# Six DRAM-to-DRAM copies of expert weights moved from SyncE's queue to ScalarE's queue

## The chip, the cores and the metric

One Trainium2 chip, of which the program uses one core. The metric is the device time of one execution in microseconds (us). Before the change three runs gave 1790.77, 1791.66 and 1792.70 us, median 1791.66.

## The reference

A stack of four layers on `x` (8 x 256 tokens of width 256), each an attention to a context of 120 rows and then a feed-forward block. Each block is added to `x` after a layer norm of its input. Cut to the two blocks that the change touches, the first feed-forward block and the last:

```python
def _L0_ffn_ref(oldx, W_in, b_in, W_out):          # 8 trees of 255 nodes
    logits = x @ W_in.T + b_in
    decisions = (logits > 0)
    acts = silu(logits)
    ...                                            # dmap: the nodes on each token's path
    return (acts * dmap).reshape(B, WIDTH) @ W_out.T

def _L3_ffn_ref(x, Wg, bg, W1, b1, W2, b2):        # 8 experts, one for each token
    probs = softmax(x @ Wg + bg)
    assignments = argmax(probs)
    h = gelu(x @ W1[e] + b1[e])
    eo = h @ W2[e] + b2[e]                         # e = assignments
    return probs[assignments] * eo
```

Between them lie attention and feed-forward blocks of layers 1 and 2 and the attention of layer 3.

## The kernel before

The eight blocks run one after the other as phases 0 to 7, each over four pairs of batches (512 tokens a pair) in a hardware loop `Fori(0, PAIRS)`. Every engine has its own instruction stream, written by hand, and the streams meet at semaphores. `x` stays in SBUF from start to end.

SyncE (SP in the profile) issues nearly all transfers, in program order. First come the loads of the first phases and the small weights of later ones (L380 to L420). Then for each attention phase it waits until the phase starts and issues masks and contexts.

The second feed-forward block (layer 2's, phase 5) uses big weights, `f1T`, `f2T`, `h1T` and `h2T`, and the last block uses expert weights. Both sets are first copied from the inputs to buffers in DRAM, and are loaded from there to SBUF when their place is free.

- `copy_f1T`, `copy_f2T`, `copy_h1T`, `copy_h2T` (1, 1, 4 and 4 MB) are issued by ScalarE (ACT) at L1203, behind its work for phase 0 and ahead of its work for phase 1. They raise the semaphore `w_copied`. SyncE waits for it (L438) before it loads them at the start of phase 2.
- `kits` (in the trace `copy_experts`), for each of 8 experts a block of 128 rows that holds its two matrices and two biases, is filled by SyncE at L457 to L462, in six copies: `w1e` in two, `w2e` in two, `b1e` and `b2e`. They stand at the end of phase 4's transfers, behind the load of `h2w` (L454) and behind the 17 MB that set the routing buffer `xbuf` to zero (L456). They raise `Hf.zeroed`. SyncE waits for it before the job loads (L470), GpSimd before it scatters the routed rows, both in phase 7.

A copy of `w1e` or `w2e` takes a slice `a[w][:, k*128:(k+1)*128, :]`, 8 experts x 128 rows x 1 KB, into rows of `kits`; `b1e` is 8 x 128 pieces of 8 bytes, and `b2e` 8 x 128 rows of 1 KB.

Phase 1, the tree block, is where ScalarE's order matters. For tree p and half c (nodes 0 to 126, nodes 127 to 254) TensorE makes logits (L1495), VectorE makes `dec` (L685), ScalarE the silu `act` (L1214), TensorE counts how many decisions agree (L1504), VectorE makes `msk` (L677) and TensorE multiplies by `woutT` (L1512). Logits lie in two sets of PSUM banks, so TensorE's stream has for tree p, ahead of its logits:

```python
if p >= 2:
    pe.wait_ge(Bf.act, i * (2 * TREES) + (2 * p - 2))
```

that is, tree 2's logits wait for both silus of tree 0. ScalarE's own stream, around the place of the change, is: the evacuations of phase 0's last `xT` (L1183, L1184), the four copies at L1203, then the silus of phase 1.

Of the kernel before, what the change touches and what calls it, by code (L numbers as in the profile page):

```python
# [17 lines left out]
B, S, D, SK = 8, 256, 256, 120  # L18
# [4 lines left out]
K2 = D // 128  # L23
# [4 lines left out]
NE = 8  # L28
# [9 lines left out]
W1, W2, B1, B2, KIT = 0, K2 * D, 2 * K2 * D, 2 * K2 * D + K2, 2 * K2 * D + K2 + D  # L38
# [31 lines left out]
def build(nc, a, out, phases=8):  # L70
# [224 lines left out]
    def sem(name):  # L295
        return es.enter_context(nc.semaphore(name))
# [4 lines left out]
    ld_h1, w_copied = sem("ld_h1"), sem("w_copied")  # L301
# [22 lines left out]
    Hf = Signals()  # L324
# [23 lines left out]
    def next_pair(i):  # L348
        return (i + 1) % PAIRS

    def rows(i, n=TT):

        return x[:, ds(TT * i, n), :]
# [6 lines left out]
    proj = {"l1x": None, "l2x": (wq2, wk2, wv2, wo2), "l3x": (wq3, wk3, wv3, wo3)}  # L360

    LD_CONST, LD_L0, LD_IN, LD_OUT, LD_L1 = 8 * 16, 5 * 16, 2 * 16, 3 * 16, 7 * 16
    W_COPIED = 4 * 16
    ZEROED = (1 + 2 * K2 + 2) * 16
    LD_L2, LD_L3X, LD_L3 = (5 + 3 + 2 * 2 + 2) * 16, 4 * 16, 2 * 16

    w_in = {w: nc.dram_tensor("copy_" + w, [m, HID], F32, kind="Internal").ap()
# [1 line left out]
    kits = nc.dram_tensor("copy_experts", [NE, 128, KIT], F32, kind="Internal").ap()  # L369
# [7 lines left out]
    def _(sp):  # L377
# [23 lines left out]
        def next_context(i):  # L401
            sp.dma_start(ctxp[:], kp(a["ctxT"][:, ds(next_pair(i) * (2 * SK), 2 * SK)])).then_inc(ctx_ready, 16)
# [18 lines left out]
        for L in LAYERS:  # L421
            if phases <= L.phase:
                break
            s = X[L.name]
            if L is L3X:
                sp.wait_ge(Ff.p1, PAIRS * HT)
                sp.dma_start(wq3[:], kp(a["wq3"])).then_inc(ld_l3x, 16)
                sp.dma_start(wk3[:], kp(a["wk3"])).then_inc(ld_l3x, 16)
                sp.dma_start(wv3[:], kp(a["wv3"])).then_inc(ld_l3x, 16)
                sp.dma_start(wo3[:], kp(a["wo3"])).then_inc(ld_l3x, 16)  # L430
            sp.wait_ge(res_done, 4 * L.phase + 1)
            sp.wait_ge(wrcp, 1)
            if L is L3X:
                sp.dma_start(wg[:], kp(a["wg"])).then_inc(ld_l3, 16)
                sp.dma_start(bgB[:], a["bg"].partition_broadcast(128)).then_inc(ld_l3, 16)
            elif L is L1X:
                sp.dma_start(m32[:], a["mask"][0:TOK, :].rearrange("(t p) k -> p t k", p=128)).then_inc(mask_ready, 16)
                sp.wait_ge(w_copied, W_COPIED)  # L438
                sp.dma_start(f1, kp(w_in["f1T"])).then_inc(ld_h1, 16)
                sp.dma_start(f2, kp(w_in["f2T"])).then_inc(ld_h1, 16)  # L440
                sp.dma_start(h1w[:], kp(w_in["h1T"])).then_inc(ld_h1, 16)
            with sp.Fori(0, PAIRS) as i:
                if L is not L3X:
                    sp.wait_ge(s.mb, i + 1)
                    sp.dma_start(m32[:], a["mask"][ds(next_pair(i) * TOK, TOK), :]
                                 .rearrange("(t p) k -> p t k", p=128)).then_inc(mask_ready, 16)
                sp.wait_ge(s.kp, i + L.c0 + 1)
                sp.wait_ge(s.vp, i + L.c0 + 1)
                next_context(i)
            if L is L2X and phases > 5:  # L450

                sp.wait_ge(mask_ready, 16 * 9)
                sp.wait_ge(res_done, 4 * 5 + 1)
                sp.dma_start(h2w[:], kp(w_in["h2T"])).then_inc(ld_h2, 16)  # L454
                sp.wait_ge(filled, 1)
                sp.dma_start(xbuf.rearrange("(p r) c -> p r c", p=128),  # L456
                             zeros[:].unsqueeze(1).broadcast_to([128, SLOTS // 128, CELL])).then_inc(Hf.zeroed, 16)  # L457
                for c, w in ((W1, "w1e"), (W2, "w2e")):
                    for k in range(K2):
                        sp.dma_start(kits[:, :, c + k * D:c + (k + 1) * D], a[w][:, k * 128:(k + 1) * 128, :]).then_inc(Hf.zeroed, 16)  # L460
                sp.dma_start(kits[:, :, B1:B1 + K2], a["b1e"].rearrange("p (e k) -> e p k", e=NE)).then_inc(Hf.zeroed, 16)
                sp.dma_start(kits[:, :, B2:B2 + D], a["b2e"].unsqueeze(1).broadcast_to([NE, 128, D])).then_inc(Hf.zeroed, 16)  # L462

        def job_weights(j, e):
            sp.dma_start(jw[:, j % NB, :], kits[ds(e, 1), :, :].rearrange("e p n -> (e p) n")).then_inc(ld_job[j % NB], 16)
# [1 line left out]
        def job_rows(j, row):  # L467
            sp.dma_start(jx[:, j % NB, :], xbuf[ds(row, 128), :]).then_inc(ld_job[j % NB], 16)

        sp.wait_ge(Hf.zeroed, ZEROED)  # L470
        sp.wait_ge(Hf.tab, 1)
        for j in range(NB):
            job_weights(j, sp.value_load(jtab[0:1, 1, j:j + 1], min_val=0, max_val=NE - 1))
# [7 lines left out]
        for load, total in ((ld_x, 16), (ld_x_rest, 16), (ld_const, LD_CONST), (ld_l0, LD_L0), (ld_in, LD_IN), (ld_out_w, LD_OUT),  # L481
                            (ld_l1, LD_L1), (ld_l2, LD_L2), (mask_ready, (0, 16 * 5, 16 * 9)[sum(phases > q for q in (2, 4))]),
                            (w_copied, W_COPIED), (ld_h1, 48 if phases > 2 else 0), (ld_h2, 16 if phases > 5 else 0), 
                            (ld_l3x, LD_L3X if phases > 6 else 0), (ld_l3, LD_L3 if phases > 6 else 0),
# [4 lines left out]
            sp.wait_ge(ld_job[b], LD_JOB * ((JOBS - 1 - b) // NB + 1))  # L489
        for b in range(NO):  # L490
            sp.wait_ge(st_job[b], 16 * ((JOBS - 1 - b) // NO + 1))
        sp.wait_ge(Hf.zeroed, ZEROED)

# [1 line left out]
    @block.gpsimd  # L497
    def _(pool):
        pool.memset(mhalf[:], -0.5)
        pool.memset(ceps[:], LN_EPS)  # L500
        pool.memset(ones[:], 1.0)
        pool.memset(zeros[:], 0.0)
        pool.drain().then_inc(filled, 1)
        pool.sem_inc(res_done, 1)

        def rstd_of(n):

            pool.wait_ge(ln_var, n)
            pool.tensor_tensor(veps[:], mv[:, :, 1], ceps[:], ALU.add)  # L509
            pool.drain()  # L510
            pool.tensor_tensor(rstd[:], veps[:], mhalf[:], ALU.pow).then_inc(ln_rstd, 1)

        rstd_of(1)

        for p in range(phases - 1):
            with pool.Fori(0, PAIRS) as i:
                if p in (4, 6):

                    if p == 4:
                        pool.wait_ge(ld_l2, LD_L2)  # L520
                    pool.wait_ge(xln_ready, 4 * p + i + 1)
                    pool.tensor_tensor(rows(i), rows(i), boB[:, p // 2 - 2, :].unsqueeze(1).broadcast_to([128, TT, D]),
                                       ALU.add).then_inc(X["l2x"].bo, 1)
                rstd_of(i + (4 * p + 2))

        pool.iota(acc[:, 0, :], pattern=[[PLACES // 128, NE]], base=0, channel_multiplier=0,
                  allow_small_or_imprecise_dtypes=True)
        pool.iota(tokc[:], pattern=[[128, NT]], base=1, channel_multiplier=1, allow_small_or_imprecise_dtypes=True)
        pool.iota(starts[:], pattern=[[PLACES, NE]], base=0, channel_multiplier=0,
                  allow_small_or_imprecise_dtypes=True)  # L530
        pool.iota(jrow[:], pattern=[[1, JOBS], [0, NE]], base=0, channel_multiplier=0,
                  allow_small_or_imprecise_dtypes=True)
        pool.memset(csum[:], 0.0)
        pool.memset(oh[:], 0.0)
        pool.memset(cells[:, :, D:CELL], 0.0)
        pool.memset(onesb[:], 1.0)
        pool.memset(tri[:], 1.0)
        pool.drain()
        pool.affine_select(tri[:], tri[:], pattern=[[1, 128]], compare_op=ALU.is_gt, fill=0.0, base=0,
                           channel_multiplier=-1)  # L540
        pool.drain().then_inc(Hf.consts, 1)

        def send(i):
            pool.wait_ge(Hf.place, i + 1)
            pool.wait_ge(Hf.cells, i + 1)
            for t in range(TT * i, TT * i + TT):
                pool.indirect_dma_start(xbuf[:], bass.IndirectOffsetOnAxis(placei[:, t:t + 1], 0), cells[:, t, :], None,
                                        bounds_check=SLOTS - 1, oob_is_err=False).then_inc(Hf.sent, 16)

        pool.wait_ge(Hf.zeroed, ZEROED)  # L550
        rstd_of(4 * 7 + 2)
        rstd_of(4 * 7 + 3)
        send(0)
        rstd_of(4 * 7 + 4)
        for i in range(1, PAIRS):
            send(i)
        for j in range(JOBS):
            pool.wait_ge(Hf.out, j + 1)
            pool.indirect_dma_start(out[:], bass.IndirectOffsetOnAxis(jtok[:, j % NO:j % NO + 1], 0), jout[:, j % NO, :],
                                    None, bounds_check=B * S - 1, oob_is_err=False).then_inc(st_job[j % NO], 16)  # L560
# [614 lines left out]
    def _(act):  # L1175
# [25 lines left out]

        for w, copy in w_in.items():
            act.dma_start(copy, a[w]).then_inc(w_copied, 16)  # L1203

        if phases > 1:
            with act.Fori(0, PAIRS) as i:
# [787 lines left out]
```

## Time and profile before

| what | us |
|---|---|
| median of three runs | 1791.66 |
| the profiled execution | 1792.70 |
| its span, first to last instruction | 1790.7 |
| TensorE busy | 1496.2 (84%) |
| ScalarE busy | 728.9 (41%) |
| phase 1 (trees), from about | 77 to 320 |
| phase 5 (layer 2's feed-forward), from about | 926 to 1310 |

The profile divides the span into 40 slices of 44.8 us and gives each engine's busy share in tenths. DMA issues are not counted as busy time of an engine: they stand in the timeline under the queue's name (ACTq, SPq), with the time for which the issue held that engine's instruction stream, which is not the time that the data took. A landing time is counted from the issue to the data's arrival.

### The profile page before, as it was taken

To read this page: it belongs to the slowest core of one execution; us is meant where nothing else is said; L and a number is where in the kernel's file an instruction comes from. 1 tells how busy PE (TensorE), PEld (TensorE's weight loads), DVE (VectorE), ACT (ScalarE), POOL (GpSimd) and SP (SyncE) were. 2 spreads that over 40 slices of the span, in tenths; PEclk is the share of its full clock that TensorE was granted. 3 is DMA by queue.
4 is the path that set the end of the run, shared out by engine and by line. 5 is a ranking of instruction groups with operands and counts; after the bars stand their busy time and mean duration, and the time that the engine had idled before them with its cause. 6 is when DMAs were issued, how large, how long until landed. Compare 5 with 4: busy or idle time off the path is not lost.

```text
span 1790.7 us, 25936 instructions
## 1 busy us (share of the span) xinstructions
PE 1496.2 (84%) x8925; PEld 1083.2 (60%) x8925; DVE 1062.5 (59%) x2273; ACT 728.9 (41%) x1214; POOL 103.0 (6%) x129
## 2 busy tenths in 40 slices
PE   6999999777779876787779999999988888888446
PEld 5665666555544443665566778787847484847345
DVE  3434434688777655778778161616167777775434
ACT  2312121456555654545442122222228474757122
POOL 0000000000000000001000000000000000000233
PEclk9999999888889997989989999999999899989579
DMA  9340000400000000000029500000000000000077
GB/s 322 104 141 0 0 0 0 158 12 11 11 0 1 1 1 12 12 3 8 11 98 342 163 1 2 1 2 2 31 6 2 6 0 5 0 5 0 22 250 232
DMA packets 56607, 88.58 MB, mean 49 GB/s; under 512 B 10419, under 2 KB 48428, under 8 KB 56366
## 3 DMA queue, kind: packets, MB, share of 16 engines
q1 hardware_dynamic: 54142, 72.08, 12.7%
q10 hardware_dynamic: 512, 11.11, 1.8%
q0 software_dynamic: 1872, 4.27, 0.6%
q8 instruction: 57, 0.93, 0.2%
q14 instruction: 24, 0.20, 0.0%
HBM read 65.74 MB, written 38.35 MB: 58 GB/s over the span
## 4 chain that ended last, share of the span: by engine, by line
issue 44%; PE 33%; DVE 9%; ACT 4%; DVEq 4%; DMA 2%; POOL 1%; ACTq 1%; SPq 1%; POOLq 0%
PE bank L1757 6%; PE bank L1758 6%; PE bank L1820 3%; PE bank L1577 3%; DVE plo L823 3%; PE bank L1597 2%; PE bank L1579 2%; DMA jx<-copy_routed 2%; PE bank L1531 2%; PE bank L1689 1%; ACT hq L1324 1%; ACTq L1323 1%; ACT phi L1265 1%; PE bank L1714 1%; DVEq L1018 1%
## 5 line engine op out<-in xcount | busy, mean ns | idle before, releaser
L823 DVE TENSOR_TENSOR plo<-e,phi 120x512 f16<-120x512 f32 x256 | 185.5, 741 | 85.7 <-ACT phi L1265 80.0
L1597 PE MATMUL bank<-Q,Kpad 128*120 128x256 f16 x1024 | 209.3, 287 | 8.6 <-ACT MBT L1257 8.6
L1271 ACT ACTIVATE e<-bank 120x512 f32<-120x512 f32 x256 | 152.7, 597 | 67.6 <-PE bank L1602 37.4
L778 DVE TENSOR_REDUCE MB<-bank 128x4 bf16<-128x480 f32 x256 | 149.9, 650 | 17.9 <-PE bank L1579 11.8
L1265 ACT ACTIVATE phi<-e 120x512 f16<-120x512 f32 x256 | 158.1, 623 | 0.0
L1577 PE MATMUL bank<-Kpad,Q 128*128 128x480 f16 x256 | 108.5, 424 | 56.3 <-issue 32.5
L1601 PE MATMUL bank<-MBT,selm 128*120 128x256 bf16 x512 | 143.8, 281 | 0.0
L1602 PE MATMUL bank<-MBT,sels 128*120 128x256 bf16 x512 | 143.8, 281 | 0.0
L1620 PE MATMUL bank<-V,phi 120*128 120x34 f16 (+1 forms) x1024 | 85.4, 176 | 56.1 <-DVE plo L823 55.0
L1597 PEld LDWEIGHTS bank<-Q,Kpad 128*120 128x120 f16 x1024 | 117.3, 138 | 10.7 <-ACT MBT L1257 10.7
L1495 PE MATMUL bank<-xT,winT 128*127 128x512 f32 (+1 forms) x256 | 114.8, 594 | 4.7 <-ACTq L1185 4.7
L1620 PEld LDWEIGHTS bank<-V,phi 120*128 120x128 f16 x1024 | 69.2, 96 | 80.0 <-DVE plo L823 71.7
L1512 PE MATMUL bank<-woutT,msk 128*128 128x256 f32 (+1 forms) x512 | 115.1, 379 | 0.0
L1577 PEld LDWEIGHTS bank<-Kpad,Q 128*128 128x128 f16 x256 | 27.7, 108 | 134.3 <-issue 73.3
L1757 PE MATMUL bank<-hah,h1w 128*128 128x512 f32 x256 | 102.4, 400 | 5.8 <-DVE hal L607 3.3
L1579 PE MATMUL bank<-MB,identb 128*128 128x480 bf16 x256 | 106.9, 418 | 0.0
L1512 PEld LDWEIGHTS bank<-woutT,msk 128*128 128x128 f32 (+1 forms) x512 | 97.2, 190 | 16.0
L1214 ACT ACTIVATE act<-bank,bin 127x512 f32<-127x512 f32 x64 | 44.0, 687 | 151.2 <-DVE dec L685 143.7
L1757 PE MATMUL bank<-hb,h2w 128*128 128x512 f32 x256 | 101.0, 395 | 0.8 <-DVE longw L1037 0.8
L1758 PE MATMUL bank<-hal,h1w 128*128 128x512 f32 x256 | 101.0, 395 | 0.0
L1758 PE MATMUL bank<-hbl,h2w 128*128 128x512 f32 x256 | 100.7, 393 | 0.0
L509 POOL TENSOR_TENSOR veps<-mv,ceps 128x4 f32<-128x4 f32 x32 | 6.4, 200 | 1573.3 <-DVEq L574 1447.0
(270 smaller groups left out, 2907.8 us busy)
## 6 DMA issues: line engine op xcount, KB each, us to landing
copy_routed<-zeros SPq DMA_DIRECT2D x1, 17028.0 KB
jw<-copy_experts SPq DMA_DIRECT2D x23, 641.0 KB, 4.8
h1w<-copy_h1T SPq DMA_DIRECT2D x1, 4096.0 KB, 18.9
h2w<-copy_h2T SPq DMA_DIRECT2D x1, 4096.0 KB, 14.1
ctxp<-in_ctxT SPq DMA_DIRECT2D x13, 240.0 KB, 2.6
jx<-copy_routed SPq DMA_DIRECT2D x23, 132.0 KB, 4.9
m<-in_mask SPq DMA_DIRECT2D x9, 240.0 KB, 2.7
copy_experts<-in_w1e SPq DMA_DIRECT2D x2, 1024.0 KB
```

The costliest lines, as they stand in the source:

```text
L778: dve.tensor_reduce(MB[:, t, h0 // 8, SK + h0 % 8:SK + h0 % 8 + 4], bank[2 + n % 4][:, 0:4 * SK].rearrange("p (h k) -> p h k", h=4), AX.X, ...
L823: dve.tensor_tensor(plo[:, u % 3, :], e32[:, u % 3, :], phi[:, u % 3, :], ALU.subtract).then_inc(s.lo, 1)
L1265: act.activation(phi[:, u % 3, :], e32[:, u % 3, :], ACT.Copy).then_inc(s.phi, 1)
L1271: act.activation(e32[:, u % 3, :], bank[2 + u % 4][0:SK, :], ACT.Exp).then_inc(s.exp, 1)
L1512: last = pe.matmul(bank[t // 2][:, (t % 2) * D:(t % 2) * D + D], msk0[0:n, p % 2, c, tok(t)], woutT[0:n, 2 * p + c, :], start=(p == 0 and ...
L1577: pe.matmul(ps, Q2[:, g, tok(t)], Kpad[:, 0, r0:r0 + 4, g, b * SK:b * SK + SK], start=True, stop=False)
L1597: pe.matmul(ps, Kpad[:, v, r, g, b * SK:b * SK + SK], Q2[:, g, qs], start=(v == 0), stop=False)
L1601: pe.matmul(ps, selm[:], MBT[:, h // 8, qs], start=False, stop=False)
L1602: last = pe.matmul(ps, sels[:, h % 8, :], MBT[:, h // 8, qs], start=False, stop=True)
L1620: pe.matmul(ps, phi[:, u % 3, cols], rhs, start=True, stop=False)
L1757: pe.matmul(ps, w, hi, start=start, stop=False)
L1758: return pe.matmul(ps, w, lo, start=False, stop=stop)
```

## The change

The six copies that fill `kits` are issued by ScalarE, right behind the four copies at L1203, and no longer by SyncE. They raise `w_copied` in place of `Hf.zeroed`, whose waits come down to the one transfer that is left on it; the wait for `w_copied` at L438 goes up from four transfers to ten. Nothing else differs.

```diff
-    W_COPIED = 4 * 16
-    ZEROED = (1 + 2 * K2 + 2) * 16
+    W_COPIED = (4 + 2 * K2 + 2) * 16
...
                 sp.wait_ge(filled, 1)
                 sp.dma_start(xbuf.rearrange("(p r) c -> p r c", p=128),
                              zeros[:].unsqueeze(1).broadcast_to([128, SLOTS // 128, CELL])).then_inc(Hf.zeroed, 16)
-                for c, w in ((W1, "w1e"), (W2, "w2e")):
-                    for k in range(K2):
-                        sp.dma_start(kits[:, :, c + k * D:c + (k + 1) * D], a[w][:, k * 128:(k + 1) * 128, :]).then_inc(Hf.zeroed, 16)
-                sp.dma_start(kits[:, :, B1:B1 + K2], a["b1e"].rearrange("p (e k) -> e p k", e=NE)).then_inc(Hf.zeroed, 16)
-                sp.dma_start(kits[:, :, B2:B2 + D], a["b2e"].unsqueeze(1).broadcast_to([NE, 128, D])).then_inc(Hf.zeroed, 16)
...
-        sp.wait_ge(Hf.zeroed, ZEROED)
         sp.wait_ge(Hf.tab, 1)
...
-        sp.wait_ge(Hf.zeroed, ZEROED)
+        sp.wait_ge(Hf.zeroed, 16)
...
-        pool.wait_ge(Hf.zeroed, ZEROED)
+        pool.wait_ge(Hf.zeroed, 16)
...
         for w, copy in w_in.items():
             act.dma_start(copy, a[w]).then_inc(w_copied, 16)
+        for c, w in ((W1, "w1e"), (W2, "w2e")):
+            for k in range(K2):
+                act.dma_start(kits[:, :, c + k * D:c + (k + 1) * D], a[w][:, k * 128:(k + 1) * 128, :]).then_inc(w_copied, 16)
+        act.dma_start(kits[:, :, B1:B1 + K2], a["b1e"].rearrange("p (e k) -> e p k", e=NE)).then_inc(w_copied, 16)
+        act.dma_start(kits[:, :, B2:B2 + D], a["b2e"].unsqueeze(1).broadcast_to([NE, 128, D])).then_inc(w_copied, 16)
```

## Rows read from the trace of the kernel before

**Rows 1.** The page: TensorE's busy time, then tenths in 40 slices of the span.

```profile
PE 1496.2 (84%) x8925; PEld 1083.2 (60%) x8925; DVE 1062.5 (59%) x2273; ACT 728.9 (41%) x1214; POOL 103.0 (6%) x129
...
PE   6999999777779876787779999999988888888446
...
DMA  9340000400000000000029500000000000000077
```

**Rows 2.** Timeline of SyncE's queue from 920 us: start, time held, instruction.

```profile
926.55 0.37 SPq L454 DMA_DIRECT2D h2w<-copy_h2T  x1
926.97 0.69 SPq L456 DMA_DIRECT2D copy_routed<-zeros  x1
927.71 64.33 SPq L460 DMA_DIRECT2D copy_experts<-in_w1e  x2
992.08 13.14 SPq L460 DMA_DIRECT2D copy_experts<-in_w2e  x2
1005.66 6.48 SPq L461 DMA_DIRECT2D copy_experts<-in_b1e  x1
1012.20 6.03 SPq L462 DMA_DIRECT2D copy_experts<-in_b2e  x1
```

**Rows 3.** SyncE's queue, what it waited for: total us, times, longest.

```profile
SPq L432 <- DVEq L646: 263.2, 1, 263.2
SPq L427 <- PE bank L1758: 246.5, 1, 246.5
```

**Rows 4.** The tile `copy_experts`: ns held at each issue, least, median, most.

```profile
L460 SPq DMA_DIRECT2D copy_experts<-in_w1e x2: 6390/32146/57901, 927.7 to 985.6; - x2
L460 SPq DMA_DIRECT2D copy_experts<-in_w2e x2: 6264/6551/6838, 992.1 to 998.4; - x2
```

**Rows 5.** Windows: length, busy (count) of PE, PEld, DVE, ACT, POOL, clock, DMA share, GB/s.

```profile
80.00:111.50 31.50, 31.50 (x107) 19.24 (x106) 13.59 (x27) 8.00 (x12) 1.21 (x2) 1.00 0.90 300
...
985.60:992.00 6.40, 3.84 (x16) 3.25 (x17) 3.75 (x9) 1.27 (x3) 0.00 (x0) 0.80 1.03 318
992.00:1018.20 26.20, 26.20 (x115) 21.62 (x114) 0.77 (x2) 4.83 (x7) 0.00 (x0) 0.98 0.53 152
1018.20:1027.00 8.80, 8.80 (x42) 7.66 (x41) 0.00 (x0) 1.97 (x2) 0.00 (x0) 1.00 0.40 121
```

**Rows 6.** Timeline of ScalarE and its queue, 76 to 81 us.

```profile
76.70 0.59 ACTq L1203 DMA_DIRECT2D copy_f1T<-in_f1T  x1
...
78.59 0.76 ACTq L1203 DMA_DIRECT2D copy_h2T<-in_h2T  x1
79.75 0.69 ACT L1214 ACTIVATE act<-bank,bin 127x512 f32<-127x512 f32 x1 [3.27 <-DVE dec L685]
80.68 0.69 ACT L1214 ACTIVATE act<-bank,bin 128x512 f32<-128x512 f32 x1 [0.24 <-PE bank L1495]
```

**Rows 7.** DMA view of 76 to 115 us: packets and MB; landing.

```profile
q10 hardware_dynamic: 224, 10.49, 79.8%
...
copy_h2T<-in_h2T ACTq DMA_DIRECT2D x1, 32.9
```

**Rows 8.** Timeline of TensorE in phase 1.

```profile
84.35 3.60 PE L1495 MATMUL bank<-xT,winT 128*127 128x512 f32 x8
```

**Rows 9.** Windows around two idle stretches of TensorE.

```profile
327.00:331.70 4.70, 0.00 (x0) 0.01 (x1) 3.92 (x6) 2.81 (x4) 0.00 (x0) 0.89 1.02 413
331.70:337.50 5.80, 5.78 (x15) 2.19 (x16) 3.95 (x6) 0.00 (x0) 0.00 (x0) 0.50 1.02 410
337.50:341.00 3.50, 3.50 (x20) 1.51 (x18) 3.48 (x7) 2.52 (x4) 0.00 (x0) 1.00 0.88 305
927.80:931.40 3.60, 0.00 (x0) 0.01 (x1) 3.07 (x7) 0.00 (x0) 0.00 (x0) 0.53 0.86 321
931.40:934.80 3.40, 3.40 (x8) 2.73 (x9) 0.00 (x0) 0.00 (x0) 0.00 (x0) 0.50 1.02 414
```

**Rows 10.** TensorE's waits from 926 to 1030 us.

```profile
PE bank L1424 <- issue: 2.3, 1, 2.3
```

## The prediction

> **What bounds the kernel now.** I read the page first. TensorE is busy 84% of the span, and its row of tenths stands at 9 in all the slices of phase 1, so a microsecond that TensorE loses there is a microsecond of the total; the DMA row is near zero between its peaks, so the DMA engines bound nothing over the whole [rows 1]. Then I read the queue that is relieved, SyncE's, in the timeline and in its waits [rows 2, 3], to see what the six copies cost where they stand now; the windows over the same stretch, to see how fast they ran and what TensorE did meanwhile [rows 5]; and last the place they move to: ScalarE's queue, what its copies look like, and who waits for ScalarE there [rows 6 to 8].
>
> **What is removed.** SyncE is held by the six issues from 927.71 to 1018.23 us, 90.5 us in all [rows 2]. It then waits 246.5 us more, for the last h1 matmul, before the next thing it has to issue [rows 3]. So 90.5 us less on that queue make that wait longer and nothing else earlier: worth 0. Do the copies disturb TensorE? From 992.0 to 1018.2 only they are in flight, and TensorE is busy all 26.20 us at a granted clock of 0.98; from 1018.2 to 1027.0 it is busy all 8.80 us [rows 5]. Nothing to gain there. Ahead of them, from 985.6 to 992.0, TensorE is idle for 2.56 us, and one of its waits near there is 2.3 us with no releaser in the profile [rows 5, 10]. The end of the zero fill runs at that time at 318 GB/s, and the fill stays. I take 0 for the removal; the upper bound is in the last rival.
>
> **What is added: six issues on ScalarE.** A plain issue costs 0.59 to 0.76 us there [rows 6]. But these copies are no plain issues [rows 2, 4]. The first `w1e` copy held SyncE for 57.9 us, the next three 6.39, 6.26 and 6.84 (the two `w2e` are the least and the most of their row, and together 13.14), `b1e` 6.48 and `b2e` 6.03. The zero fill, itself accepted in 0.69 us, was ahead of the first. So an issue is accepted at once when nothing long is being queued, and otherwise holds its engine until the one ahead has been queued, and that in turn goes only as fast as data drain once the queue is full.
>
> How much fits? The five 1 MB copies are 5.25 MB. From 992.0 to the end 26.2 us at 152 GB/s and 8.8 at 121 moved, 3.98 + 1.06 = 5.04 MB [rows 5]. So when the second `w1e` issue returned at 992.0, 0.2 MB had moved, and of the copy before it about 0.84 MB was left: some 820 of its 1,024 rows of 1 KB fit into the queue; the issue returns when the rest of the copy ahead has gone. When the last issue returned at 1018.2, 1.06 MB was left, just its own copy.
>
> On ScalarE the same sequence stands behind the four weight copies. These are 224 packets for 10.49 MB [rows 7], so they take little room in a queue that counts pieces, which is why they held ScalarE so briefly. But they take long: the last lands 32.9 us after its issue, at 78.59 + 32.9 = 111.5 us [rows 6, 7], with the DMA engines 0.90 busy from 80.0 to 111.5 [rows 5]. A queue is drained in order, so nothing behind them moves until then. Step by step:
>
> - 79.4: the first `w1e` copy is issued, accepted in about 0.65 us, as the zero fill was. 80.0.
> - The second `w1e` is held until all but 820 rows of the first are gone: that needs the weight copies done (111.5) and 0.2 MB more, at 1.05 MB in 6.3 us some 1.2 us. 112.7.
> - The other four are held as before, where they took from 992.0 to 1018.2, 26.2 us. 138.9.
>
> ScalarE is free at 138.9 and not at 79.4; 59.5 us of a stream that has work to do.
>
> **Who waits.** Behind the six issues stand the silus of tree 0, which started at 79.75 and 80.68 [rows 6]. VectorE's `msk` for tree 0 waits for them, and so does TensorE's block of logits for tree 2, which ran at 84.35 [rows 8]. TensorE has logits for trees 0 and 1 and one count to do, and that is done by 84.35: from there it stands. The two silus, 0.69 us each and 0.1 for the hand-over, end at 140.3, and the logits for tree 2 start at 140.4. That is 140.4 - 84.35 = **56.0 us** later. After that every engine has the order it had, and TensorE is full again, so nothing is won back in phase 1; nor later, since no later work stands on a time that doesn't shift with it (all early loads landed long before, and SyncE had waited 263.2 us for phase 2 to start [rows 3]; the new copies land at about 138.9 + 8.8 = 147.7 us, before it needs `w_copied`).
>
> **The clock.** TensorE idles for 56 us. After idle stretches of 4.7 and 3.6 us the granted clock stood at 0.50, that is 1.2 of 2.4 GHz, for the next 5.8 and 3.4 us of full work, and then rose to 1.00 [rows 9]. Half of these times is lost: 2.9 and 1.7 us. In before that clock was 1.00 in all of this stretch [rows 5]. I take the middle, **2.3 us**.
>
> **Sum.** 56.0 + 2.3 = 58.3 us. The profiled execution took 1792.7 us; 1851.0. It was 1.0 us above the median of its runs (1791.66), so for a median I say **1850.0 us**. A difference under 0.2% (3.6 us) I call no change.
>
> **The rivals.**
>
> - *ScalarE's issues are short: no back-pressure there.* For it: all its copies so far were accepted in under 0.8 us, with 10 MB in flight [rows 6, 7]. Then the six cost 6 x 0.62 = 3.7 us, tree 0's silus end at 79.4 + 3.7 + 1.5 = 84.6 against 84.35: +0.3 us, 1792. Against it: those copies were few large pieces, while each of these is 1,024 small ones, and SyncE was held by the very same ones. The Trainium skill ("DMA: Bandwidth & Descriptors", section "Issuing engines are not separate DMA queues") says for this case that a second issuing engine saves only the time to initiate the transfer, "which is usually small relative to the DMA itself"; by that rule the total would be this rival's, some 1792, and the trace speaks against it [rows 2], with holds of 6 to 58 us.
> - *ScalarE's queue is deeper by a copy.* The 0.84 MB is measured on SyncE's queue alone. With room for one copy more, each issue returns a copy (6.4 us) earlier: 1850.0 - 6.4 = 1843.6. For it nothing is seen; the two queues may differ.
> - *Each issue waits until everything ahead has moved.* Then ScalarE is free only at 111.5 + 6 x 6.4 = 149.9, the logits start at 151.4, 67.0 later, and with 2.9 for the clock it is 1861.6. Against it: at 992.0 and at 1018.2 about a copy was still outstanding.
> - *Faster.* The first rival holds, and phase 5 gets back what it lost around the copies: 2.6 us of idle TensorE from 985.6 to 992.0 and some 1.7 us of half clock behind it (0.80 in that window [rows 5], priced as above): 1792.7 + 0.3 - 4.3 - 1.0 = 1787.7. It decides only if ScalarE is held for less than the 3.0 us between the end of tree 0's second silu (80.68 + 0.69 = 81.37) and 84.35, and if the copies and not the fill made that idle time. The copies didn't start to move in bulk until about then. Improbable.
>
> That the change doesn't do its work is no case: the kits are in place long ahead of the jobs in either order.
>
> **How the numbers follow.** Forecast 0.70, deeper queue 0.12, waits for all 0.08, short issues 0.08, faster 0.02. The forecast's own bounds: the clock 0.6 us either way; the queue's share of the first copy, from none of it fitting (+5) to all of it (-1); and the weight copies' end, whose last engines set 111.5 while the mean DMA share in 80 to 111.5 is 0.90, so ScalarE's engines may be through up to 3 us earlier. Together 1845 to 1856. Taking in both neighbours gives 1842 to 1862, which leaves out 0.10 with the cases of no change. Slower 0.90, same 0.08, faster 0.02.
>
> **What would show it.** In the profile after, ScalarE's queue from 79.4 us: issues of about 0.6, 33, 6.4, 6.4, 6.8 and 6.3 us, in sum 59. TensorE idle for about 56 us from 84.8, ended by `act`, then a clock of 0.50 for 3 to 6 us. Phase 1's pace from tree to tree afterwards as before, and phases 2 to 7 the same in length. SyncE has no `copy_experts` writes around 930 to 1018, and TensorE there is as it was. Wrong would be: issues all under 1 us (then the queue isn't limited by pieces); a first long hold other than 33 us (then the weight copies don't stand in front); phases after that shorter or longer by more than 2 us (then the copies did disturb phase 5).

## The result and the profile after

| | median us | runs |
|---|---|---|
| before | 1792.18 | 4 (1790.77 to 1798.93) |
| after | 1849.44 | 4 (1846.72 to 1851.64) |

The ratio is 1.0311, 95% interval 1.0282 to 1.034: 57 us slower, where 58 were forecast (1850.0). The profiled execution after took 1848.59 us, its span is 1846.5 against 1790.7. Line numbers after are a few lower than before (L1494 is what was L1495, L1213 what was L1214).

The page after, TensorE's busy time and the tenths of TensorE and of the DMA engines. It answers to [rows 1]:

```profile
PE 1498.2 (81%) x8918; PEld 1081.7 (59%) x8925; DVE 1062.2 (58%) x2273; ACT 728.7 (39%) x1214; POOL 104.2 (6%) x129
...
PE   7709999977776986777877899999988888888446
...
DMA  9360000040000000000007700000000000000067
```

TensorE is busy for the same time as before (1498.2 against 1496.2 us) in a longer span. The third slice (92 to 138 us, the slices are 46.2 us long here) has gone from 9 to 0. In the same slice the DMA row has risen from 4 to 6, and of its peak in the middle, 2, 9 and 5 before, 7 and 7 are left.

The timeline of ScalarE and its queue, with the issues that answer to [rows 2] and [rows 6]:

```profile
78.45 0.81 ACTq L1196 DMA_DIRECT2D copy_h2T<-in_h2T  x1
79.29 31.23 ACTq L1199 DMA_DIRECT2D copy_experts<-in_w1e  x2
110.55 12.41 ACTq L1199 DMA_DIRECT2D copy_experts<-in_w2e  x2
122.99 6.23 ACTq L1200 DMA_DIRECT2D copy_experts<-in_b1e  x1
129.25 6.00 ACTq L1201 DMA_DIRECT2D copy_experts<-in_b2e  x1
135.51 2.42 ACT L1213 ACTIVATE act<-bank,bin 127x512 f32<-127x512 f32 x4 [59.20 <-issue]
```

The same tile by least, median and most ns of one issue:

```profile
L1199 ACTq DMA_DIRECT2D copy_experts<-in_w1e x2: 1287/15600/29912, 79.3 to 80.6; - x2
```

The last weight copy is accepted at 79.26. The first `w1e` copy held ScalarE 1.29 us, the second 29.9, the two `w2e` copies 6.2 each, `b1e` 6.23 and `b2e` 6.00. ScalarE is free at 135.25 and does the four silus that had piled up back to back, 2.42 us. The DMA view from 108.5 us to 110.52, when the second `w1e` issue came back, shows how much of the kit copies had started by then:

```profile
DMA packets 174, 0.16 MB, mean 80 GB/s; under 512 B 16, under 2 KB 174, under 8 KB 174
```

That is 158 rows of 1 KB and 16 short packets. So 866 of the 1,024 rows of the first `w1e` copy were still outstanding, where the prediction had 820.

TensorE, and what ended its idle time:

```profile
83.76 0.60 PE L1503 MATMUL bank<-dec,anc 127*127 127x512 bf16 x2
136.83 5.17 PE L1494 MATMUL bank<-xT,winT 128*127 128x512 f32 x8 [52.48 <-ACT act L1213]
141.84 0.60 PE L1503 MATMUL bank<-dec,anc 127*127 127x512 bf16 x2
142.28 3.62 PE L1511 MATMUL bank<-woutT,msk 127*128 127x256 f32 x16
145.73 3.60 PE L1494 MATMUL bank<-xT,winT 128*127 128x512 f32 x8
```

The block of 8 at 136.83 is the logits for tree 2, which ran at 84.35 before [rows 8]. Its one new wait in phase 1 is 52.5 us, and `act` ended it. The block took 5.17 us where the same one takes 3.60. The windows say why; the columns are those of [rows 5], the granted clock is the third from the right:

```profile
84.30:110.00 25.70, 0.05 (x1) 0.00 (x0) 0.00 (x0) 0.00 (x0) 0.00 (x0) 0.58 0.89 293
110.00:136.80 26.80, 0.00 (x0) 0.00 (x0) 0.48 (x1) 1.29 (x3) 0.00 (x0) 0.50 0.54 158
136.80:139.80 3.00, 2.97 (x4) 1.42 (x5) 0.93 (x2) 1.13 (x2) 0.00 (x0) 0.50 0.55 170
139.80:143.00 3.20, 3.20 (x11) 1.72 (x11) 1.28 (x2) 1.37 (x2) 0.00 (x0) 0.99 0.46 139
...
1040.00:1047.00 7.00, 4.18 (x18) 3.48 (x19) 4.10 (x10) 1.51 (x3) 0.00 (x0) 0.81 0.85 263
1047.00:1073.00 26.00, 26.00 (x115) 21.45 (x114) 0.42 (x1) 4.83 (x7) 0.00 (x0) 0.99 0.00 1
```

The clock fell to 0.50 while TensorE stood, and the first 3.0 us of work were done at that level, 1.2 GHz. The last two rows are windows of phase 5, 54.5 us later than 985.6 to 1018.2 in [rows 5]: TensorE is busy all the time from 1047 on, as it was beside the copies, and in the window ahead of that it is idle for 2.8 us, as it was (2.6). What SyncE waited for shows where the 90 us of holds on that queue went:

```profile
SPq L426 <- PE bank L1757: 337.6, 1, 337.6
```

The wait for the last h1 matmul grew from 246.5 to 337.6 us [rows 3]: all the time saved on SyncE became waiting.

### The profile page after: what moved, and what is told of

The parts are those of the page before. It is cut to its first block, busy times and chain, and to the rows that moved or that the text cites. A ratio compares the mean times of both kernels' runs of the same rounds, so it can differ in the third digit from the quotient of the medians.

```text
span 1846.5 us, 25928 instructions
## 1 busy us (share of the span) xinstructions
PE 1498.2 (81%) x8918; PEld 1081.7 (59%) x8925; DVE 1062.2 (58%) x2273; ACT 728.7 (39%) x1214; POOL 104.2 (6%) x129
## 4 chain that ended last, share of the span: by engine, by line
issue 49%; PE 30%; DVE 9%; DVEq 4%; ACT 3%; DMA 2%; POOL 1%; SPq 1%; ACTq 1%; POOLq 1%
PE bank L1756 6%; PE bank L1757 6%; PE bank L1819 3%; DVE plo L816 3%; PE bank L1576 2%; PE bank L1596 2%; PE bank L1578 2%; DMA jx<-copy_routed 2%; PE bank L1530 1%; DVEq L1011 1%; ACT phi L1264 1%; PE bank L1601 1%; PE bank L1688 1%; PE bank L1600 1%; PE bank L1646 1%
## 5 line engine op out<-in xcount | busy, mean ns | idle before, releaser
L1494 PE MATMUL bank<-xT,winT 128*127 128x512 f32 (+1 forms) x256 | 116.4, 600 | 57.2 <-ACT act L1213 52.5
L1576 PE MATMUL bank<-Kpad,Q 128*128 128x480 f16 x256 | 107.8, 421 | 55.8 <-issue 32.0
L1213 ACT ACTIVATE act<-bank,bin 127x512 f32<-127x512 f32 x64 | 43.6, 687 | 205.8 <-DVE dec L678 139.5
L1494 PEld LDWEIGHTS bank<-xT,winT 128*127 128x127 f32 (+1 forms) x256 | 48.7, 192 | 108.7 <-issue 54.2
L670 DVE SCALAR_TENSOR_TENSOR msk<-bank,tgt,act 127x512 f32<-127x512 f32 x64 | 45.1, 746 | 100.8 <-ACT act L1213 53.3
```

Source lines behind the costliest of these rows:

```text
L1494: last = pe.matmul(bank[2 + 2 * (p % 2) + c][0:n, :], winT[:, k, w0:w0 + n], xT[:, k, :], start=(k == 0), stop=(k == K2 - 1))
L1576: pe.matmul(ps, Q2[:, g, tok(t)], Kpad[:, 0, r0:r0 + 4, g, b * SK:b * SK + SK], start=True, stop=False)
```

## The experiments

Each run was timed beside runs of the kernel before on the same chip. Those have medians of 1792.9 (with e1, e3, e4, e5), 1794.08 (e2, e6, e7, e8) and 1793.37 (e9, e10). Where no ratio is given, there was a single run.

**e1_sp_early: the same six copies early, on a queue that has time.**

```diff
         sp.dma_start(attnm[:], ...).then_inc(ld_l2, 16)
+        for c, w in ((W1, "w1e"), (W2, "w2e")):
+            for k in range(K2):
+                sp.dma_start(kits[:, :, c + k * D:c + (k + 1) * D], a[w][:, k * 128:(k + 1) * 128, :]).then_inc(Hf.zeroed, 16)
+        sp.dma_start(kits[:, :, B1:B1 + K2], ...).then_inc(Hf.zeroed, 16)
+        sp.dma_start(kits[:, :, B2:B2 + D], ...).then_inc(Hf.zeroed, 16)
```

> The six copies are issued by SyncE, right behind its early loads (some 44 us into the span), and none by ScalarE. They move in the same part of the kernel as after the change, but hold a queue that has nothing to do until 321 us. My theory, that the loss is the time for which the issues hold ScalarE's stream: 1792 us as before, within 0.2%, with TensorE in phase 1 as before. Rival, that it is the DMA traffic beside phases 0 and 1: slower by tens of us. Rival, that phase 5 had lost time to these copies: faster by up to 4 us.

Measured: 1794.31 us, ratio 1.0009 (0.9992 to 1.0026): no change. SyncE's timeline:

```profile
42.30 6.78 SPq L423 DMA_DIRECT2D copy_experts<-in_w1e  x2
49.13 12.37 SPq L423 DMA_DIRECT2D copy_experts<-in_w2e  x2
61.54 6.21 SPq L424 DMA_DIRECT2D copy_experts<-in_b1e  x1
67.79 5.97 SPq L425 DMA_DIRECT2D copy_experts<-in_b2e  x1
```

From the third issue on the holds are those that ScalarE had (12.4 for the two `w2e`, 6.2, 6.0); the two `w1e` copies, with no slow copies in front, took 6.8 us and not 31.2. So the holds belong to the copies, and not to the engine that issues them. They cost nothing here, where nothing is queued behind them until phase 2. Bringing the traffic forward cost nothing either, and taking it out of phase 5 gained nothing. Most of it runs here beside phase 0; e7 and e9 put as much beside phase 1.

**e3_one and e4_two: one copy, two copies.** The others stay on SyncE in phase 5.

```diff
+    ON_ACT = 1        # e4_two: 2
...
             act.dma_start(copy, a[w]).then_inc(w_copied, 16)
+        for k in range(ON_ACT):
+            act.dma_start(kits[:, :, W1 + k * D:W1 + (k + 1) * D], a["w1e"][:, k * 128:(k + 1) * 128, :]).then_inc(w_copied, 16)
```

> ScalarE issues only the first w1e copy, SyncE the other five where they were. Theory: one issue of about 1 us behind the weight copies, which the 3.0 us between tree 0's silus and the logits for tree 2 cover: 1792 us, no stall of TensorE. The rival of equal costs gives 1801; if a single copy is held behind the weight copies already, TensorE stands some 26 us: 1820.

> ScalarE issues only the two w1e copies behind the four weight copies, SyncE the other four where they were. Theory: the first is accepted in about 1.3 us, the second holds ScalarE until the weight copies have moved and a fifth of the first, some 30 us, to 110.6 and not 135.3. TensorE then stands 24.7 us less: 1849.4 - 24.7 = 1825 us. A rival in which every copy costs the same (a sixth of 57 us each, 9.5) gives 1811; one in which the hold comes only with all six gives 1792.

Measured: one copy 1792.43 us, two copies 1824.08. ScalarE's queue and TensorE's tree 2 block with one copy:

```profile
79.24 1.29 ACTq L1206 DMA_DIRECT2D copy_experts<-in_w1e  x1
80.80 1.27 ACT L1217 ACTIVATE act<-bank,bin 127x512 f32<-127x512 f32 x2 [4.63 <-PE bank L1498]
```

TensorE in the same run:

```profile
84.04 3.60 PE L1498 MATMUL bank<-xT,winT 128*127 128x512 f32 x8
```

and with two (the fence gives both issues in one row):

```profile
81.35 31.38 ACTq L1206 DMA_DIRECT2D copy_experts<-in_w1e  x2
```

TensorE in the same run:

```profile
114.32 5.46 PE L1498 MATMUL bank<-xT,winT 128*127 128x512 f32 x8 [27.83 <-ACT act L1217]
```

The first copy is accepted in 1.29 us, and the 3.0 us of room in front of tree 2 cover that: TensorE has no wait. The second costs TensorE 27.8 us of waiting and 1.9 in the slow block behind it (5.46 for 3.60); the total of this single run is 31 us longer. Both waits are as forecast. The cost of the sequence isn't spread evenly over it, and a count of issues times a mean would have been wrong for both.

**e5_kits_first: what stands in front.** The six are issued ahead of the four weight copies, else as in the changed kernel.

```diff
+        for c, w in ((W1, "w1e"), (W2, "w2e")):
+            ...
+        act.dma_start(kits[:, :, B2:B2 + D], ...).then_inc(w_copied, 16)
         for w, copy in w_in.items():
             act.dma_start(copy, a[w]).then_inc(w_copied, 16)
-        for c, w in ((W1, "w1e"), (W2, "w2e")):
-            ...
```

> All ten copies on ScalarE, the six kit copies ahead of the four weight copies. Theory: nothing slow stands in front, so the second w1e copy is held some 3 us and not 30, the next four 6.2 each, and f1T about 6 until b2e is queued; ScalarE is free at about 111 us in place of 135, total 1849.4 - 24 = 1825 us (1820 to 1830). A rival in which the hold is made by the six copies alone, whatever stands in front, gives 1849.

Measured: 1816.89 us. ScalarE's queue:

```profile
76.73 2.97 ACTq L1197 DMA_DIRECT2D copy_experts<-in_w1e  x2
79.73 12.37 ACTq L1197 DMA_DIRECT2D copy_experts<-in_w2e  x2
...
104.47 1.29 ACTq L1201 DMA_DIRECT2D copy_f1T<-in_f1T  x1
...
108.29 2.42 ACT L1213 ACTIVATE act<-bank,bin 127x512 f32<-127x512 f32 x4 [31.79 <-issue]
```

TensorE in the same run:

```profile
109.61 5.29 PE L1494 MATMUL bank<-xT,winT 128*127 128x512 f32 x8 [25.07 <-ACT act L1213]
```

The two `w1e` copies cost 2.97 us together in place of 31.2: their long hold was that of the weight copies in front. The other four are held as ever, and TensorE still waits 25.1 us, less than half of the 52.5. The estimate was 8 us too high, and the time lies outside the 1820 to 1830 that it allowed. `f1T` was accepted in 1.29 us, not 6, so ScalarE was free at 108.0 and not at 111: what stood ahead of the `b2e` rows were the 8-byte pieces of `b1e`, and these go fast (e8 has 2.6 us for 1,024). The rest is within what single runs differ by (the kernel before beside it: 1788.93 to 1800.22).

**e7_big_pieces and e8_small_pieces: bytes or pieces.** Extra work behind the weight copies of the kernel before, into scratch buffers: five copies of 1 MB in few pieces, or six of 8 KB in 1,024 pieces each.

```diff
+        for n in range(5):                                   # e7_big_pieces
+            act.dma_start(big[n], a["f1T"]).then_inc(w_copied, 16)
...
+        for n in range(6):                                   # e8_small_pieces
+            act.dma_start(small[n][:, :, 0:K2], a["b1e"].rearrange("p (e k) -> e p k", e=NE)).then_inc(w_copied, 16)
```

> The kernel before, and behind the four weight copies ScalarE issues five more copies of 1 MB, contiguous, of f1T into scratch buffers in DRAM (extra work whose results nobody reads). Same bytes in the same place as the five large kit copies, but in few large pieces. Theory, that the queue is full by the number of pieces: each is accepted in 0.6 to 0.8 us, 3.2 us in all, TensorE loses under 1 us: 1792 to 1793 us. Rival, that it is full by bytes: held until 10 MB have moved, tens of us, about 1840.

> The kernel before, and behind the four weight copies ScalarE issues six copies like b1e, 1,024 pieces of 8 bytes each into scratch buffers (extra work whose results nobody reads): 48 KB in all. Theory of pieces: the first is accepted in about 1.3 us, the second held some 30 us, to about 110, because the pieces can't move before the weight copies. Each of the next four is then held by what a copy of 1,024 pieces takes: 6 us if making or queuing the pieces limits (total about 1848), 1 to 3 us if their transfer does (total about 1830). Rival of bytes: nothing is held, 1793.

Measured: 5.24 MB in big pieces 1792.51 us, 48 KB in small ones 1832.54 us. The tile of the extra copies (ns held: least, median, most) and TensorE's tree 2 block, with big pieces:

```profile
L1206 ACTq DMA_DIRECT2D extra<-in_f1T x5: 611/614/626, 79.4 to 82.0; - x5
```

TensorE in the same run:

```profile
84.21 3.68 PE L1498 MATMUL bank<-xT,winT 128*127 128x512 f32 x8
```

and with small ones:

```profile
L1206 ACTq DMA_DIRECT2D extra<-in_b1e x6: 1242/2556/29736, 78.8 to 117.8; - x6
```

TensorE in the same run:

```profile
121.76 5.26 PE L1498 MATMUL bank<-xT,winT 128*127 128x512 f32 x8 [37.70 <-ACT act L1217]
```

A hundredth of the bytes costs 38 us and the full bytes nothing. The most of the small ones, 29.7 us, is the hold behind the weight copies; the median is 2.6 us, against 6.2 for an issue that has a 1 MB copy of the same count ahead of it. So the number of pieces, and not the bytes, says whether an issue is held, and what is ahead says for how long. For the 1 KB rows that is their transfer: they keep the DMA engines at a share of 0.54 to 0.57 through all the holds of 6 us. For the small ones it isn't shown, since the share in e8 is only 0.21 from 110 to 120 us: their 2.6 us may be the making of the pieces.

**e6_rows_first: half the DMA engines?** The same pieces, with the 128 rows as the outer dimension.

```diff
-                act.dma_start(kits[:, :, c + k * D:c + (k + 1) * D], a[w][:, k * 128:(k + 1) * 128, :]).then_inc(w_copied, 16)
+                act.dma_start(kits[:, :, c + k * D:c + (k + 1) * D].rearrange("e p n -> p e n"),
+                              a[w][:, k * 128:(k + 1) * 128, :].rearrange("e p n -> p e n")).then_inc(w_copied, 16)
```

(and so for `b1e` and `b2e`)

> The changed kernel with the same six copies and the same pieces, but each written with the 128 rows as its outer dimension and the 8 experts as the inner, so that the slowest dimension is 128 and not 8. Theory: with 8 outer entries a copy uses only half of the 16 DMA engines (DMA share 0.54 while only they run), so that half of the places in the queue and half of the rate are lost. With 128 the DMA share is near 1, a copy takes some 3.3 us, the hold of the third comes in place of that of the second, and the last four take 3.3 each: ScalarE free at about 120 us in place of 135, total 1849.4 - 15 = 1834 us. If the order of the dimensions is of no matter: 1849.

Measured: 1836.98 us. The tile `copy_experts` and a window while only these copies run:

```profile
L1199 ACTq DMA_DIRECT2D copy_experts<-in_w1e x2: 651/14116/27581, 80.8 to 81.5; - x2
L1199 ACTq DMA_DIRECT2D copy_experts<-in_w2e x2: 4068/4780/5491, 109.1 to 113.2; - x2
...
L1202 ACTq DMA_DIRECT2D copy_experts<-in_b2e x1: 3832/3832/3832, 123.8 to 123.8; - x1
```

The window, with the columns of [rows 5]:

```profile
115.00:121.00 6.00, 0.00 (x0) 0.00 (x0) 0.00 (x0) 0.00 (x0) 0.00 (x0) 0.50 1.13 210
```

The DMA share rose to 1.13, from 0.54 in the changed kernel: with 8 as the slowest dimension only half of the engines work. The Trainium skill has the rule ("DMA: Bandwidth & Descriptors", section "Why a DMA increments its semaphore by 16 and not by 1"): a copy uses the largest number of engines up to 16 that divides the slowest dimension that isn't 1 on both of its sides. That much agrees. Two of my numbers don't. The rate rose only to 210 GB/s, from 158 to 170 (the windows after, with shares of 0.54 and 0.55), so the holds came down to 3.8 to 5.5 us and not to 3.3. And the long hold, 27.6 us, stayed at the second issue. That the queue has places for each engine does fit: when the third issue returned (113.15) and when the fourth did (118.7), some 1,510 and 1,430 rows were outstanding by the DMA view, against 866 with half of the engines. But 64 rows and 10 pieces of a weight copy for each engine would then have fit at the second issue, so the full queue isn't simply a count in which a 64 KB piece takes the place of one row. How much of the queue the weight copies' pieces take was not measured.

**e9_one_per_tree: the same engine, spread out.** One copy behind the silus of each of trees 0 to 5 of the second pair.

```diff
                         act.activation(act0[...], bank[...], ACT.Silu, ...).then_inc(Bf.act, 1)
+                    if p < 6:
+                        with act.If(i == 1):
+                            ...      # the p-th of the six copies
```

> The six kit copies on ScalarE as in the changed kernel, but not in a row: one behind the silus of each of the trees 0 to 5 in the second pair of phase 1, 7.3 us apart, with the weight copies long through. Theory: a copy of this kind moves in 6.2 us, so each finds the one ahead of it queued and is accepted in about 1.3 us, in ScalarE's idle 5.7 us per tree: no stall of TensorE, 1792 to 1794 us. Rival, that these issues cost ScalarE their 6 us wherever they stand: ScalarE needs 6.2 + 1.6 us per tree against 7.3, with the wait for msk in between up to some 10 us more in all: 1800 us or above.

Measured: 1793.15 us, ratio 0.9999 (0.9987 to 1.001): no change. ScalarE's queue, and its idle time around the issues:

```profile
141.86 1.29 ACTq L1214 DMA_DIRECT2D copy_experts<-in_w1e  x1
144.28 0.69 ACT L1208 ACTIVATE act<-bank,bin 127x512 f32<-127x512 f32 x1 [1.81 <-DVE dec L678]
...
145.29 0.71 ACTq L1214 DMA_DIRECT2D copy_experts<-in_w1e  x1
...
149.16 2.02 ACTq L1214 DMA_DIRECT2D copy_experts<-in_w2e  x1
155.48 0.69 ACT L1208 ACTIVATE act<-bank,bin 127x512 f32<-127x512 f32 x1 [5.71 <-DVE dec L678]
```

Held 1.3, 0.7, 2.0, 1.2, 0.7 and 0.7 us, all within ScalarE's idle time, and TensorE's 52.5 us wait is gone. (The first three stand only 3.4 and 3.9 us apart, not 7.3; the third was held 2.0.) So the cost was neither ScalarE as the issuing engine nor phase 1, but six issues in a row, and behind four slow copies: with those out of the way 25.1 of the 52.5 us stay (e5), with the row broken up nothing does.

**e2_fill_early and e10_fill_alone: is there anything to win in phase 5?** The zero fill goes to SyncE's early loads, with the six copies (e2) or without (e10).

```diff
+        sp.wait_ge(filled, 1)                                 # behind attnm
+        sp.dma_start(xbuf.rearrange(...), zeros[:]...).then_inc(Hf.zeroed, 16)
```

> As the kernel with the six copies on SyncE behind the early loads, and the 17 MB zero fill of the routing buffer moved there too, behind them. Phase 5 then runs without either. What is left of the rival that phase 5 loses time to this traffic: TensorE's 2.6 us of idle time and the half clock behind it near the end of its first pair, up to 4.3 us: 1788 us. My theory, that this idle time isn't made by the transfers: 1792 us, within 0.2%.

(In the kernel that ran the fill stood ahead of the six copies and not behind them; SyncE was held 86 us by the first two and had time for that.)

> The kernel before with only the 17 MB zero fill moved, from phase 5 to SyncE's early loads; the six copies stay at phase 5. In the run with both moved, TensorE's wait of 2.3 us without a releaser in phase 5 was gone and 1.3 us of the gap there with it. If the fill made it: gone here too, and the total 1 to 3 us under the kernel before. If the copies had a part in it: a wait stays there.

Measured: 1791.17 us, ratio 0.9987 (0.9978 to 0.9996), and 1791.28 us, ratio 0.9985 (0.9974 to 0.9996). The timeline of TensorE in phase 5 of e1, where the fill is still running at that place:

```profile
989.65 0.39 PE L1758 MATMUL bank<-hal,h1w 128*128 128x512 f32 x1
992.31 1.09 PE L1424 MATMUL bank<-ident,xln 128*128 128x128 f32 x8 [2.27 <-issue]
...
994.35 0.49 PE L1757 MATMUL bank<-hb,h2w 128*128 128x512 f32 x1 [0.83 <-DVE longw L1037]
```

and the same of e10, where the fill was moved and the six copies are through by then:

```profile
983.47 0.39 PE L1758 MATMUL bank<-hal,h1w 128*128 128x512 f32 x1
983.70 1.03 PE L1424 MATMUL bank<-ident,xln 128*128 128x128 f32 x8
...
986.84 0.49 PE L1757 MATMUL bank<-hb,h2w 128*128 128x512 f32 x1 [1.99 <-DVE longw L1037]
```

The wait of 2.27 us with no releaser is gone, as it is in e2. It stands, at 2.3 us, in the profiles of all the other kernels here. They all have the fill in phase 5, some with the six copies behind it (before, e7) and some without (after, e1, e9). The next wait is longer (1.99 for 0.83); from the last h1 block to the first `h2w` block it is 3.37 us where it was 4.70. So the fill made it, and I had expected that no transfer did. The gain is within the 0.2% that I call no change, but its interval excludes none: some 2 to 3 us, of which this place shows 1.3. What of the fill delays TensorE is open. Of all kernels here e2 and e10 are the fastest, and without the change.

## Why the prediction was right

*The removal is worth 0.* Right within what the runs can tell: e1 takes the copies out of phase 5 as the change does and gains nothing, and SyncE's saved time became waiting. The upper bound of the last rival, however, was partly real: some idle time there was made by transfers, but by the fill, which the change leaves where it is (e10).

*An issue is held until the copy ahead is queued.* Right, shown from four sides: the first costs TensorE nothing (e3), the second pays for what is in front of it (e4, e5), pieces and not bytes fill the queue (e7, e8), and with time between them none is held for long (e9). Two expectations that were built on it missed: e5 by 8 us, and in e6 the long hold stayed at the second issue. How the places of the queue are counted is open.

*Step by step on ScalarE.* The steps were right and the sizes 3.7 us too high in sum. The second `w1e` copy was accepted at 110.5 and not 112.7. The rows of the first `w1e` copy that had to go before were nearly right (158 for 200); the end of the weight copies was put too late. The prediction took their landing, 111.5, but the first kit rows started at 109.0, as the bound of "up to 3 us earlier" allowed for. From 107.5 to 109.0 only three packets start, each under 512 bytes: the last large pieces of the weight copies were under way by then. The last four took 24.7 us and not 26.2. ScalarE was free at 135.25 for 138.9.

*Who waits.* Right in every link: tree 0's two silus, the first of the four that had piled up, then tree 2's logits. 136.83 - 84.35 = 52.5 us for the forecast 56.0.

*The clock.* 3.0 us of work at 0.50 cost 1.6 us (5.17 against 3.60) for the forecast 2.3.

*Nothing later.* Phase 2 starts 54.1 us later (its mask load goes from 321.20 to 375.26), in line with 52.5 + 1.6. The span is 55.8 longer. The other 1.7 us arose in small steps on the way, and between runs of one kernel here the totals differ by more than that; they have no cause that these runs show.

*How close the number is.* That is partly luck. The two terms that were forecast, 56.0 + 2.3, measured 52.5 + 1.6, 4.2 us less. The small steps gave 1.7 of that back, and the rest lies in which runs are compared: the two profiled executions differ by 55.9 us, the medians by 57.3.

*The rivals.* Short issues: what e7 does, and it needs big pieces. The sentence of the Trainium skill ("DMA: Bandwidth & Descriptors", section "Issuing engines are not separate DMA queues") that the time to initiate a transfer is "usually small" holds for e7 and e9 and for the first copy; the other five held ScalarE for 54.5 us. A deeper queue would have been 1843.6, waiting for everything 1861.6, and the measured 1849.4 is at neither. The holds decide it better than the total: with room for one copy more the long hold would have come at the third issue, and it came at the second; and that one returned with 866 rows of the copy ahead outstanding, so it didn't wait for everything. The sign "a first long hold other than 33 us" came out at 29.9, by the early end of the weight copies and not by their absence (e5).

## What to carry to other kernels

Moving a DMA issue to another engine moves its hold too: read how long the issue held its old queue, and ask what the new engine has to do in that time. The hold isn't the instruction's own price; it is that of what is still in front of it in that queue, so many pieces behind slow copies were the worst case here, and one issue at a time with work between was free (e9). Here the queue whose next task was hundreds of microseconds away was the right place, however busy it looked in the timeline (before, e1).

## What was not expected of the hardware

- With the 16 engines used (share 1.13) the strided copies moved at 210 GB/s, against 158 to 170 with half of them (0.54 to 0.55).
- A 17 MB fill from SBUF to DRAM delayed TensorE, which waited for nothing that the profile shows, by 1.3 us at one place. The kernel's total without it was 0.13% and 0.15% lower (e2, e10).
